# Finer GpSimd passes, another issuing engine for the score operands, and moved turns and products in a fused transformer layer

## The reference

```python
x = _L0(x)      # one finite-difference step, then maximum(x, 0)
# L1, adaptive transformer block, 16 heads of 32
x = _ln(x) * (1.0 + scale) + shift
q, k, v = (x @ Wq + bq), (x @ Wk + bk), (x @ Wv + bv)
scores = einsum('bhqd,bhkd->bhqk', q / sqrt(32), k) + attention_bias
probs = softmax(where(mask, -inf, scores))
x = x + (einsum('bhqk,bhkd->bhqd', probs, v) @ Wo + bo)
h = _ln(x) * g2 + beta2
x = x + _gelu2(h @ W1 + b1) @ W2 + b2
# L2, adapter with one expert per image, then a layer norm
hidden = gelu(x @ down_W.T + down_b) @ expert_W[idx].T ...
x = _ln(hidden @ up_W.T + up_b + x) * ln_gamma + ln_beta
# L3, rotation of channel pairs by the angles theta and phi
```

## Time and profile before

| | us |
| --- | --- |
| median of 3 runs | 4827.24 |
| lowest, highest | 4826.14, 4832.1 |
| profiled execution, time | 4833.72 |
| profiled execution, span | 4831.9 |

### The profile page before, as it was taken

One profiled execution on the slowest core, in us unless ns is written; L12 is line 12 of the kernel. 1 busy time (PEld: TensorE's weight loads), 2 busy tenths in 40 slices (PEclk: granted clock), 3 DMA queues, 4 the chain that ended last, 5 costly groups with the idle time before them and its releaser, 6 DMA issues.

```text
span 4831.9 us, 70103 instructions
## 1 busy us (share of the span) xinstructions
PE 4177.3 (86%) x25329; PEld 3062.8 (63%) x25720; DVE 2653.0 (55%) x5144; ACT 2039.9 (42%) x4344; POOL 798.3 (17%) x477
## 2 busy tenths in 40 slices
PE   6994679898888989898988989898989989898977
PEld 3442457676666757676766767676767667676755
DVE  8993445555545555555555555555555555555453
ACT  0001455445444454444444444544454444445441
POOL 0002022302002020302021121202020210203021
PEclk9997899999999999999999999999999999998998
DMA  3325667676766666676757666666757576666643
GB/s 121 106 97 153 191 205 242 192 227 185 214 178 207 214 185 202 188 229 178 228 175 212 198 206 209 200 193 173 234 180 226 179 208 203 203 212 177 206 127 100
DMA packets 398996, 914.01 MB, mean 189 GB/s; under 512 B 46000, under 2 KB 67296, under 8 KB 398656
## 3 DMA queue, kind: packets, MB, share of 16 engines
q1 hardware_dynamic: 389696, 891.67, 60.9%
q10 hardware_dynamic: 8448, 16.78, 0.9%
q0 software_dynamic: 512, 1.05, 0.1%
HBM read 715.94 MB, written 58.79 MB: 160 GB/s over the span
## 4 chain that ended last, share of the span: by engine, by line
PE 63%; DMA 8%; SPq 6%; DVE 5%; ACT 4%; issue 3%; POOL 1%; another core or an unknown queue 0%; POOLq 0%; ACTq 0%; DVEq 0%
PE bank L861 44%; DMA stack<-parts 8%; PE bank L928 7%; SPq L581 5%; PE bank L919 4%; PE bank L949 4%; ACT probT L746 2%; PE bank L920 2%; PE bank L882 1%; PE bank L1000 1%; PE bank L935 1%; DVE prob L1106 1%; SPq L508 1%; DVE parts L1098 1%; ACT prob L738 1%
## 5 line engine op out<-in xcount | busy, mean ns | idle before, releaser
L746 ACT ACTIVATE probT<-bank 128x512 f32<-128x512 f32 x1024 | 610.1, 596 | 1844.6 <-PE bank L928 1841.9
L1106 DVE CUSTOM_DVE_ANT_0 prob<-bank,prob 128x512 f32<-128x512 f32 x1024 | 704.3, 688 | 869.2 <-remote 391.7
L861 PE MATMUL bank<-zT,w 128*128 128x512 f32 x3072 | 817.5, 416 | 51.6 <-issue 44.9
L861 PE MATMUL bank<-w,gparts 128*128 128x512 f32 x3072 | 781.8, 403 | 55.2 <-DVE gparts L1161 54.7
L928 PE MATMUL bank<-ident,prob 128*128 128x128 f32 x4096 | 642.7, 281 | 138.3 <-ACT probT L746 87.3
L738 ACT ACTIVATE prob<-prob,low 128x512 f32<-128x512 f32 x1024 | 733.0, 716 | 45.8 <-DVE low L1106 45.3
L861 PEld LDWEIGHTS bank<-zT,w 128*128 128x128 f32 x3072 | 591.0, 195 | 190.4 <-issue 59.0
L928 PEld LDWEIGHTS bank<-ident,prob 128*128 128x128 f32 x4096 | 514.4, 145 | 297.5 <-issue 96.6
L919 PE MATMUL bank<-stack 128*128 128x512 f32 x1024 | 514.4, 502 | 214.1 <-DMA stack<-parts 98.5
L861 PEld LDWEIGHTS bank<-w,gparts 128*128 128x128 f32 x3072 | 571.4, 189 | 174.0 <-issue 61.3
L861 PE MATMUL bank<-xT,w 128*128 128x512 f32 x1536 | 419.6, 425 | 10.2 <-DVE xT L1083 8.1
(11 more groups left out here) (175 smaller groups left out, 5021.7 us busy)
## 6 DMA issues: line engine op xcount, KB each, us to landing
w<-split_w SPq DMA_DIRECT2D x720, 512.0 KB, 4.4
prob<-in_fside_Bx16xSxS SPq DMA_DIRECT2D x512, 512.0 KB, 4.2
stack<-parts SPq DMA_DIRECT2D x1024, 128.0 KB, 6.5
split_w<-w SPq DMA_DIRECT2D x48, 512.0 KB, 3.3
field<-in_x SPq DMA_DIRECT2D x16, 1024.0 KB, 5.3
x<-total ACTq DMA_DIRECT2D x16, 1024.0 KB, 5.9
xin<-x SPq DMA_DIRECT2D x16, 1024.0 KB, 10.4
out<-tok SPq DMA_DIRECT2D x16, 1024.0 KB, 7.7
```

Source lines behind the costliest of these rows:

```text
L746: act.activation(probT[:, m % TURNED, :], turned[:], ACT.Copy).then_inc(turn_copied, 1)
L861: mm = te.matmul(dst, stat(hs, k), mov(hm, k), start=start and n == 0, stop=stop and n == count - 1)
L1106: v.tensor_tensor_reduce(prob[:, m % PROBS, :], score[:], prob[:, m % PROBS, :], -1.0, MIN_START, ALU.add, ALU.min, low[:, i:i + 1]).then_ ...
```

## The change

1. GpSimd's passes over a whole image are cut in four, a quarter each, with own slots (`BO_AT`, `B2_AT`, `UP_B_AT`, and `gamma`, `beta` and sines one slot after the quarter's up product); norm and rotation on VectorE follow by quarters.
2. `load_stack` moves from SyncE to ScalarE, after the other work of its slot; for group 1 it begins one slot later.
3. The input turns go to bank `proj`, into slots 36, 38, 40 and 42, and TensorE no longer waits for the low part before the slot's own turn.
4. The projections of group 1 move from slots 0 and 2 to 7 and 9, behind the output product; the value products from 50, 52, 54, 56 to 49, 51, 54, 58, the up products from 51, 51, 53, 53 to 52, 53, 55, 56.
5. Two of the four raises of `zT` (scale by `g2`, add `beta2`) go from ScalarE to VectorE.
6. `scale_context` runs one slot later, but for the last group of an image.

```diff
-QK_AT = ((45, 47), (0, 2), (16, 18), (30, 32))
+QK_AT = ((45, 47), (7, 9), (16, 18), (30, 32))
+STACK_AT = (9, 10, 9, 9)
 CTX_LAST_AT, O_AT, Z_TURN_AT = 1, 3, 8
 FF1_AT, FF2_AT = 11, 14
-LOAD_X_AT, STATS_AT, ADAPT_AT, EXPERT_AT, X_TURN_AT = 8, 18, 26, 20, 36
+LOAD_X_AT, STATS_AT, ADAPT_AT, EXPERT_AT = 8, 18, 26, 20
+X_TURN_AT = (36, 38, 40, 42)
 Y_AT, Y_TURN_AT, DOWN_AT, EXPERT_MM_AT = 44, 46, 48, 50
-V_AT, UP_AT = (50, 52, 54, 56), (51, 51, 53, 53)
-V_BANK, UP_BANK = (1, 2, 3, 2), (3, 0, 1, 0)
-NORM_AT, ROTATE_AT = 55, 62
+V_AT, UP_AT = (49, 51, 54, 58), (52, 53, 55, 56)
+V_BANK, UP_BANK = (1, 2, 1, 2), (3, 0, 3, 0)
+BO_AT, B2_AT, UP_B_AT = (43, 44, 50, 51), (13, 15, 17, 19), (45, 46, 47, 48)
+ROTATE_AT = (57, 59, 61, 62)
 MASK_AT = (49, 53, 57, 61)
 CTX_AT = 57
...
-                def load_stack(gg, j):
...
-                        i = s % 16
-                        if 16 - LEAD - HG <= i < 16 - LEAD and n < B and (t // 16 + 1) < G * B:
-                            load_stack(t // 16 + 1, i - (16 - LEAD - HG))
...
-                                pool.wait_ge(z_ready, a + 1)
-                                pool.tensor_tensor(res[:], res[:], bcast(row["b2"]), ALU.add).then_inc(res_biased, 1)
+                            if s in B2_AT:
+                                q = B2_AT.index(s)
...
+                                add_row(res[:, q, :], tok[:, q, :], "up_b", y_biased)
                             for q in range(TB):
...
                                     root(var_y, rstd_y, TB * a + q + 1, q)
-                            if s == NORM_AT:
-                                pool.wait_ge(normed, 2 * a + 1)
-                                pool.tensor_tensor(tok[:], tok[:], bcast(row["gamma"]), ALU.mult).then_inc(normed, 1)
-                                pool.wait_ge(normed, 2 * a + 2)
-                                pool.tensor_tensor(tok[:], tok[:], bcast(row["beta"]), ALU.add).then_inc(affine, 1)
-                                pool.wait_ge(affine, a + 1)
-                                quads = tok[:].rearrange("p t (q c) -> p (t q) c", c=4)
-                                crossed = res[:].rearrange("p t (q c) -> p (t q) c", c=4)
-                                for h in range(2):
-                                    sine = scal[:, a, 4 + 2 * h:5 + 2 * h]
-                                    pool.tensor_scalar(crossed[:, :, 2 * h], quads[:, :, 2 * h + 1], sine, None, ALU.mult).then_inc(sined, 1)
-                                    pool.tensor_scalar(crossed[:, :, 2 * h + 1], quads[:, :, 2 * h], sine, -1.0, ALU.mult, ALU.mult).then_inc(sined, 1)
+                            for q in range(TB):
+                                if s == UP_AT[q] + 1:
+                                    pool.wait_ge(normed, TB * a + q + 1)
+                                    pool.tensor_tensor(tok[:, q, :], tok[:, q, :], row["gamma"][:], ALU.mult).then_inc(gained, 1)
+                                    pool.wait_ge(gained, TB * a + q + 1)
+                                    add_row(tok[:, q, :], tok[:, q, :], "beta", affine)
+                                    pool.wait_ge(affine, TB * a + q + 1)
+                                    quads, crossed = (t[:, q, :].rearrange("p (n c) -> p n c", c=4) for t in (tok, res))
+                                    for h in range(2):
+                                        sine = scal[:, a, 4 + 2 * h:5 + 2 * h]
+                                        pool.tensor_scalar(crossed[:, :, 2 * h], quads[:, :, 2 * h + 1], sine, None, ALU.mult).then_inc(sined, 1)
+                                        pool.tensor_scalar(crossed[:, :, 2 * h + 1], quads[:, :, 2 * h], sine, -1.0, ALU.mult, ALU.mult).then_inc(sined, 1)
...
+                            if s in BO_AT:
+                                q = BO_AT.index(s)
                                 pool.wait_ge(x_turned, KB * c + KB)
-                                pool.tensor_tensor(xin[c % 2][:], xin[c % 2][:], bcast(row["bo"]), ALU.add).then_inc(xin_biased, 1)
+                                add_row(xin[c % 2][:, q, :], xin[c % 2][:, q, :], "bo", xin_biased)
...
                 def x_hi_part(b, k):
                     act.wait_ge(x_turned, KB * b + k + 1)
-                    act.activation(xT[0][:, k, :], (turned if b else sums[k])[:], ACT.Copy).then_inc(x_hi, 1)
+                    act.activation(xT[0][:, k, :], (proj if b else sums[k])[:], ACT.Copy).then_inc(x_hi, 1)
+
+                def load_stack(gg, j):
+
+                    if gg:
+                        act.wait_ge(score_full, 16 * (gg - 1) + 12 + j + 1)
+                    act.wait_ge(qk_hi, 2 * gg + 2)
+                    act.wait_ge(qk_lo, 2 * gg + 2)
+                    for quad, (q, step) in enumerate(((0, 2), (1, 1), (0, 3), (1, 2))):
+                        act.dma_start(stack[DH * quad:DH * (quad + 1), j, :, :].bitcast(F32),
+                                     parts[DH * j:DH * (j + 1), q:q + step + 1:step, :].bitcast(F32)).then_inc(stack_in[j], 16)
...
-                        if c < B and X_TURN_AT <= s < X_TURN_AT + KB:
-                            x_hi_part(c, s - X_TURN_AT)
+                        if c < B and s in X_TURN_AT:
+                            x_hi_part(c, X_TURN_AT.index(s))
...
+                                    if k % 2 == 0:
+                                        act.wait_ge(z_turned, KB * a + k + 1)
+                                    if k % 2:
+                                        act.wait_ge(z_raised, KB // 2 * a + k // 2 + 1)
+                                    else:
+                                        if k:
+                                            act.wait_ge(z_lo, KB * a + k - 1)
+                                        act.activation(gel[:, 0, :], sums[k][:], ACT.Identity, bias=col["beta2"][:, k:k + 1],
+                                                       scale=col["g2"][:, k:k + 1]).then_inc(z_wide, 1)
+                                        act.wait_ge(z_wide, KB // 2 * a + k // 2 + 1)
                                     act.activation(zT[0][:, k, :], gel[:, k % 2, :], ACT.Copy).then_inc(z_hi, 1)
...
+                        gg = t // 16 + 1
+                        if n < B and gg < G * B and 0 <= s % 16 - STACK_AT[gg % G] < HG:
+                            load_stack(gg, s % 16 - STACK_AT[gg % G])
                         split_hi(t)
...
+                    if filled["x"]:
+                        te.wait_ge(x_lo, filled["x"])
...
                 def input_turn(b, k):
                     if k == 0:
                         te.wait_ge(x_ready, b + 1)
-                        if b:
-                            te.wait_ge(qk_full, 2 * G * b)
-                    turn(turned if b else sums[k], xin[b % 2], k, x_turned)
+                    if b:
+                        await_proj()
+                        filled["x"] = KB * b + k + 1
+                    turn(proj if b else sums[k], xin[b % 2], k, x_turned)
...
-                        if c < B and X_TURN_AT <= s < X_TURN_AT + KB:
-                            te.wait_ge(turn_copied, block_entry(t))
-                            input_turn(c, s - X_TURN_AT)
+                        if c < B and s in X_TURN_AT:
+                            input_turn(c, X_TURN_AT.index(s))
...
-                            if c < B and X_TURN_AT <= s < X_TURN_AT + KB:
-                                te.wait_ge(x_lo, KB * c + s - X_TURN_AT + 1)
                             turn_block(t)
...
                     if s in (Z_TURN_AT + 1, Z_TURN_AT + 2):
                         for k in (2 * (s - Z_TURN_AT - 1), 2 * (s - Z_TURN_AT - 1) + 1):
                             v.wait_ge(z_hi, KB * a + k + 1)
                             v.tensor_tensor(zT[1][:, k, :], gel[:, k % 2, :], zT[0][:, k, :].bitcast(F32), ALU.subtract).then_inc(z_lo, 1)
+                    if s in (Z_TURN_AT, Z_TURN_AT + 1):
+                        k = 2 * (s - Z_TURN_AT) + 1
+                        v.wait_ge(z_turned, KB * a + k + 1)
+                        if k > 2:
+                            v.wait_ge(z_lo, KB * a + k - 1)
+                        v.tensor_scalar(gel[:, 1, :], sums[k][:], col["g2"][:, k:k + 1], col["beta2"][:, k:k + 1], ALU.mult, ALU.add).then_inc(z_raised, 1)
...
-                    if s == NORM_AT:
-                        for q in range(TB):
+                    for q in range(TB):
+                        if s == UP_AT[q] + 1:
                             v.wait_ge(rstd_y, TB * a + q + 1)
-                            if q < TB - 1:
-                                link.mark(normalise(tok, res, q))
-                            else:
-                                normalise(tok, res, q).then_inc(normed, 1)
...
+                            normalise(tok, res, q).then_inc(normed, 1)
+                        if s == ROTATE_AT[q]:
+                            v.wait_ge(sined, TB * (TB * a + q + 1))
```

(7 more changed lines are left out.)

87 lines of the change are left out of this document (30 added, 57 removed).

## The result

| | us | ratio to before, 95% interval |
| --- | --- | --- |
| before, median of 4 runs | 4826.69 (4815.19 to 4832.1) | |
| after, median of 4 runs | 4918.11 (4909.39 to 4936.27) | 1.0198 (1.0159 to 1.0236) |
| after, span of the profiled execution | 4907.6 (before 4831.9) | |

The change costs 2.0%, where 1.7% less was forecast, and the time lies above the range. In the profiled executions the first copy comes at 482.4 us (475.9 before), the first image takes 183.0 (199.3), the last image, to its last copy, 245.9 (234.4), and from there to the end 170.9 us pass (175.1); together 2.5 us less, where 15 were forecast. What was lost was lost in the fourteen images between, 78 us, some 6 us in each instead of a gain of 4.9.

A forecast was written before the change was run, and what follows sets the result against it. TensorE was taken to set the time nearly everywhere, so only filling idle stretches or removing waits gains. Terms summed to -4.9 us an image, -69 over fourteen, -84 in all: 4743 us from a median of 4827.2, range 4650 to 4845.

The forecast's parts named there:

- Slots 52 to 64: From slot 51's copy: 44.7 us for today's 45.6, landing taken as 5.6; with a lower-clock value product +0.9 an image.
- ScalarE's lag: ScalarE issuing stack pieces makes its copies late for TensorE's turns; 0.5 us charged at each of three places.
- VectorE's wait for the root of quarter 2: New wait before `normalise`, GpSimd reaching the root only after two quarters and a mask step; some 4 us lost on VectorE.
- Input turns: Slots 36 to 43: waits for copies and emptying go in the projection bank, turns leave odd slots; -4.4 us an image.
- Context scale: VectorE's waits in slots 17 and 33 go, -3.5 us, with 0.5 back for lag in slots 25 to 28; -3.0 an image.
- Projections of group 1: Leaving slots 1 and 2 gives -1.9 us; arriving in slots 7 and 9 makes slots 3 to 16 together +1.6.
- Slots 49 to 51: One 3.0 us product more, two small ones and some idle time less; +1.4 us an image.
- Outside the steady images: First image about -5 us, last image -4, the end, with norm and rotation pipelined by quarters, -6.
- ScalarE hides its issues: Rival, chance 0.30: DMAs issue while activations run, last piece lands 5 us earlier; -13.4 us an image, 4624, middle 4684.
- ScalarE becomes the bound: Rival, chance 0.10: issuing costs more than ScalarE's slack, 0.9 us a DMA; +11.2 us an image, 4969 (4843 at 0.75).
- The turns and context edits do nothing: Rival, chance 0.06: the gains of 3.5 and 4.4 us reappear as the next wait; +3 us an image, 4854.
- Break-even: Rival, chance 0.12: landing stays 7.4 us, GpSimd's quarters take 5.6, slot 11's clock gain is missing; -0.3 an image, 4823.

The follow-up runs named there:

- e7: e6 with ScalarE issuing the stack pieces of each image's first group only (slots 57 to 60), SyncE the others; 4711.98 us, ratio to before 0.9738.
- e6: Changed kernel with GpSimd's four roots ahead of its quarter passes, rotations later, and SyncE issuing the stack pieces again; 4693.0 us, ratio to before 0.9687.
- e12: e11 with the four weight loads freed by the last value product issued after the last stack piece of slot 61; 4685.59 us, ratio to before 0.9682.
- e11: e6 with the last value product in slot 56 in place of slot 58; 4711.7 us, ratio to before 0.9748.
- e1: Changed kernel with GpSimd's four roots ahead of the quarter passes and VectorE's rotations one or two slots later; 4836.67 us, ratio to before 0.9994.
- e10: e6 with ScalarE issuing four small unused DMAs wherever it issued a stack piece in the changed kernel; 4691.57 us, ratio to before 0.9707.
- e9: e6 with SyncE issuing each stack piece one slot later; 4822.8 us, ratio to before 0.9976.
- e4: Kernel before with only the input turns moved to the projection bank in slots 36, 38, 40 and 42; 4794.39 us, ratio to before 0.9897.
- e5: Kernel before with only the context scale of groups 1 to 3 one slot later; 4784.77 us, ratio to before 0.988.
- e8: e6 with the projections of group 1 back in slots 0 and 2; 4692.65 us, ratio to before 0.9693.

## Why the prediction was wrong

**What bounds the kernel: right.** TensorE sets the time where it has products, and slots 58 to 64 are where time is to be had.

**Slots 52 to 64, the step that failed first.** The chain was named well: it was the size of its terms. All times here count from the end of slot 51, and each forecast has the 1.8 us that I added for a value product at the lower clock (the earlier trace rows give 1.5). The turn of slot 58 was to come by 25.8 and came at 26.7: GpSimd took 12.3 us to the root and not 11.5, and the product ran 5.47 us and not 4.8. Then ScalarE was to issue the last piece by 38.8 and did by 35.6, since it hides its issues (charged 4.1 to 4.8 a slot, measured 2.8 to 3.6). The prediction says four such slots there; its own 37 fits three of them behind that turn, and the trace shows three, with the first piece already issued in slot 58, before the stall. But TensorE got the last piece at 46.6 (2578.32 - 2531.73), where I had 43.8: 11.0 us after its last issue ended (2567.37), and not 5.0. The end is at 50.6 (2582.30 - 2531.73) against 46.5 forecast: 3.2 us won by ScalarE, 6.0 lost in the landing and 1.3 behind it. The landing is the mis-sized term that turned the sum: 5.6 was taken "nearer to the earlier trace rows", because the pieces leave the queue of the weights. That does not free them from the loads: in e7 against e6 the last piece is issued 2.5 us earlier and is complete only 0.4 us earlier. What helped was the order, the loads behind the pieces (e12: the last piece takes 4.3 us to land, in e11 8.8).

**ScalarE's lag, the step that failed most.** I had charged 0.5 us for each of three places, 1.5 in all. e1 against e6 puts the move at 9.7 us an image: 2.4 in slots 11 to 16, 1.8 in 36 to 43, 4.0 in 44 to 48, 1.3 in 58 to 64. I asked what ScalarE's issues cost ScalarE (next to nothing in time, e10). I did not ask who needs the pieces to have landed, and when they may start. On SyncE, which waits for little else, a piece leaves when the last scores of the old group free it; in ScalarE's code it stands behind the exponential and the copy of the slot, in slots 25 to 28 and 41 to 44 0.8 to 3.8 us later in the mean (e1 against e6). The landing itself grows too. The last piece of slots 41 to 44, which `q_hi` in slot 46 waits for, is complete 6.7 us after the copy of slot 44 begins in e6, 11.1 in e1 and 11.4 in e9; of the 4.4 us between e6 and e1, 1.0 is the later issue and 3.4 the longer landing. Why it lands more slowly there stays open; e9 shows that it takes no DMA on ScalarE. The cover that I had named, ScalarE's chain, held. The cover that I had not named, the time between landing and `q_hi` in slot 46 and the scores in slots 13 to 15, was thin, and it went.

**The wait that I saw and did not weigh.** VectorE's wait for the root of quarter 2 was forecast as 4 us and measured as 5.40, in its place and for its reason. But I had set it off against stalls of the kernel before that would go. With the roots in front (e1) the wait is gone and the time falls by 2.0%. That order has a price of its own: in e6 TensorE waits 8.7 us for VectorE's minimum in slots 59 to 64, which waits behind rotations as e12 shows, and from the last copy to the end 180.3 us pass (170.9 in the changed kernel). A wait that a text can name in advance is an edit to ask for, not a term to carry.

**Input turns, -4.4 forecast.** The waits on `xT` went; 1.0% by e4, 3.2 to 3.5 us an image. The 1.5 us that came back in slot 43 stood beside GpSimd's whole add, and in e4 alone.

**Context scale, -3.0 forecast.** Right: slots 18 and 34 give 3.5 us, the image is 3.1 us shorter and the time 1.2% by e5.

**Projections of group 1.** I had -1.9 for slots 1 and 2 and, for slots 3 to 16, +1.6 with the clock's gain of 1.6 in slot 11. e8 shows the move itself to be worth nothing. The product of slot 11 did get faster (3.03 us in the mean of the eleven images, 4.76 before), but it takes 3.60 with the projections back in slots 0 and 2 (e8) and 3.44 in e6, so that the move explains little of it.

**Slots 49 to 51.** +1.4 forecast, +0.6 measured.

**Outside the steady images.** -15 forecast, -2.5 measured, and no term came near but the end's: first copy +6.5 (forecast 0; ScalarE's issues ahead of it, as e7 shows), first image -16.3 (-5), last image +11.5 (-4), end -4.2 (-6).

**The rivals.** "ScalarE hides its issues" had the mechanism right, but its last piece did not land 5 us earlier: it was issued earlier and landed later. "ScalarE becomes the bound" gave 4843 to 4969, where the time is, and is refuted as a mechanism: a DMA costs 0.6 us and the time is covered. "The turns and context edits do nothing" falls by e4 and e5. Break-even came nearest by its terms, landing not better and GpSimd's quarters dearer (5.6 and 5.3 measured, 5.6 in this rival, 5.0 forecast), but none of the rivals had a landing that grows, and that was the case. Of the signs named for a wrong forecast two came: a landing over 7 us, and slots 52 to 64 over 48.

**The page that spoke against the change.** The trace had the DMA engines 0.80 busy there, and the landing went up from 7.4 to 9.1 us in slots 58 to 64, from 4.2 to 6.3 in slots 19 to 31. The Trainium skill ("DMA: Bandwidth & Descriptors", section "Issuing engines are not separate DMA queues") says that DMAs of several issuers interleave on the same 16 engines and that only issue time is saved; the trace agrees, and so does e7. I had let it change the landing by 1.8 us at most; that a piece could take longer still to land does not follow from the page, and was measured.

## What to carry over

Before a DMA moves to another engine, write down two times for each transfer: when the old issuer could start it and when the first reader (or the next writer of its source) needs it landed. If the slack is thin, the issuer that waits for little else should keep it, and large loads that nobody needs soon go behind it; issue time on a half-idle engine was the smaller question here. The time from issue to landing is no constant of the transfer: it moved with the issue.

When bulk work is cut in pieces, order the short results that others wait for (here a root of 0.6 us) ahead of the pieces; and of a wait that you can name in advance, ask first whether an order without it exists. Then look at what the new order pushes back: here the rotations, the next wait.

## What was not expected of the hardware

DMA issues on ScalarE run beside its activations (2560.47 within the row of 2560.10 above); four of them leave 0.9 to 1.7 us of it idle, not 2.5.

In slots 57 to 60 a transfer of 128 KB landed in 2.6 to 4.3 us where SyncE had issued it ahead of the 512 KB loads (e12, the means of the four pieces over eleven images) and in 7.7 to 8.8 us where it came after them (e11). In slots 25 to 28 and 41 to 44 an issue 2.7 to 4.4 us later made the landing itself longer too (e9 5.1 to 7.5 us, e6 3.2 to 6.2), so that the delay counted more than once.

VectorE's pair of rotation steps on a quarter took 2.53 us beside GpSimd's `gamma` and `beta` and 1.19 us eight microseconds later, when GpSimd was at the end of a `beta` and at a sine step:

```profile
2552.30 2.53 DVE L1216 SCALAR_TENSOR_TENSOR tok<-tok,scal,res 128x256 f32<-128x256 f32 x2
...
2560.16 1.19 DVE L1216 SCALAR_TENSOR_TENSOR tok<-tok,scal,res 128x256 f32<-128x256 f32 x2
```

The step of 4.99 us in e4 stood beside a whole pass of GpSimd of 4.58 us in the same way. That GpSimd's accesses are the cause was not tried apart.
